# An adaptive-norm feed-forward kernel: the scaling of the down product goes from VectorE to ScalarE and GpSimd

## What is computed

```python
y = conv1d(x, weight, groups=4, padding=4) + cond @ c_weight.T + bias   # 128 x 32 x 512
def qlinear(x, w): return fake_quant(x, axis=-1) @ fake_quant(w, axis=1).T
h = silu(qlinear(y, w_gate)) * qlinear(y, w_up)      # inner width 1376
out = x + qlinear(h, w_down)                         # back to width 512
```

## Time and profile before

| | us |
|---|---|
| median of 3 runs | 334.96 (332.92 to 336.75) |
| the profiled execution, its own time | 334.56 |
| its span, first to last instruction | 332.8 |
| mean granted TensorE clock | 0.981 of full |

### The profile page before, as it was taken

One profiled execution on the slowest core, in us unless ns is written; L12 is line 12 of the kernel. 1 busy time (PEld: TensorE's weight loads), 2 busy tenths in 40 slices (PEclk: granted clock), 3 DMA queues, 4 the chain that ended last, 5 costly groups with the idle time before them and its releaser, 6 DMA issues.

```text
span 332.8 us, 4922 instructions
## 1 busy us (share of the span) xinstructions
PE 298.8 (90%) x1728; PEld 178.5 (54%) x1728; DVE 260.1 (78%) x426; ACT 210.2 (63%) x251; POOL 199.9 (60%) x200
## 2 busy tenths in 40 slices
PE   1989699989639699999999999999999999999934
PEld 1989699986325244444444544444444445444411
DVE  0699998996357678888888888788887888888830
ACT  1057889496975856556766667766577656676530
POOL 1266856793663555776666776657766667756541
PEclk9999799999998999999999999999999999999997
DMA  7899834500000823565445754446654456544482
GB/s 290 325 308 390 306 137 164 220 2 2 0 0 19 196 43 76 136 153 137 110 106 121 141 152 124 108 107 139 152 137 106 108 125 147 147 115 106 111 196 109
DMA packets 59032, 46.36 MB, mean 139 GB/s; under 512 B 47520, under 2 KB 47648, under 8 KB 58112
## 3 DMA queue, kind: packets, MB, share of 16 engines
q1 hardware_dynamic: 58720, 45.43, 48.8%
q10 hardware_dynamic: 288, 0.62, 0.6%
HBM read 26.12 MB, written 8.39 MB: 104 GB/s over the span
## 4 chain that ended last, share of the span: by engine, by line
PE 72%; DVE 14%; ACT 5%; DMA 4%; POOL 1%; issue 1%; SPq 0%; POOLq 0%; ACTq 0%; DVEq 0%
PE bank L765 40%; PE bank L778 21%; PE bank L670 7%; DVE y_part L563 3%; DVE y_mem L554 3%; DMA w_mem<-w_mem 3%; DVE gu_max L531 2%; DMA small_sb<-cond_ctx_bias 2%; ACT y_mem L426 2%; DVE h_max L621 1%; PE bank L726 1%; ACT slab L485 1%; DVE d_max L541 1%; ACT w_mem L494 1%; ACT sg_mem L480 1%
## 5 line engine op out<-in xcount | busy, mean ns | idle before, releaser
L387 POOL TENSOR_TENSOR sg_mem<-sg_mem,gu_scale_row 128x512 f32<-128x512 f32 (+1 forms) x96 | 111.5, 1162 | 88.2 <-ACT sg_mem L480 88.2
L765 PE MATMUL bank<-wgu_t,xq_t 128*128 128x512 bf16 (+1 forms) x768 | 155.8, 359 | 3.8 <-DVE slab L615 3.8
L765 PEld LDWEIGHTS bank<-wgu_t,xq_t 128*128 128x128 bf16 x768 | 75.0, 98 | 82.7 <-DVE slab L615 5.0
L480 ACT ACTIVATE sg_mem<-sg_mem,x_scale 128x512 f32<-128x512 f32 (+1 forms) x96 | 64.3, 672 | 44.9 <-DVE sg_mem L605 44.8
L778 PE MATMUL bank<-wd_t,w_mem 128*128 128x512 bf16 (+1 forms) x352 | 82.8, 385 | 8.7 <-DMA w_mem<-w_mem 8.7
L605 DVE TENSOR_TENSOR sg_mem<-bank,gu_scale_row 128x512 f32<-128x512 f32 (+1 forms) x96 | 60.3, 629 | 31.6 <-PE bank L765 31.6
L615 DVE SCALAR_TENSOR_TENSOR slab<-bank,x_scale,sg_mem 128x512 f32<-128x512 f32 (+1 forms) x96 | 66.5, 692 | 10.0 <-POOL sg_mem L387 9.6
L485 ACT ACTIVATE slab<-slab,h_inv 128x1376 f32<-128x1376 f32 x32 | 46.2, 1443 | 37.2 <-DVE h_inv L521 37.2
L778 PEld LDWEIGHTS bank<-wd_t,w_mem 128*128 128x128 bf16 (+1 forms) x352 | 34.6, 99 | 48.4 <-DMA w_mem<-w_mem 10.0
L670 PE MATMUL bank<-toeplitz,slab 128*128 128x192 f32 (+1 forms) x320 | 54.5, 326 | 0.0
L670 PEld LDWEIGHTS bank<-toeplitz,slab 128*128 128x128 f32 x320 | 51.7, 205 | 0.0
(11 more groups left out here) (44 smaller groups left out, 132.1 us busy)
## 6 DMA issues: line engine op xcount, KB each, us to landing
xo_mem<-x SPq DMA_DIRECT2D x32, 256.0 KB, 3.3
out<-xo_mem SPq DMA_DIRECT2D x32, 256.0 KB, 2.9
w_mem<-w_gate_up SPq DMA_DIRECT2D x10, 512.0 KB, 6.7
slab<-x_blocks SPq DMA_DIRECT2D x4, 1024.0 KB, 8.9
slab<-x_blocks SPq DMA_DIRECT2D x3, 1088.0 KB, 5.9
w_mem<-w_down SPq DMA_DIRECT2D x4, 688.0 KB, 6.4
slab<-x_blocks SPq DMA_DIRECT2D x1, 576.0 KB, 5.1
toeplitz<-taps_wide ACTq DMA_DIRECT2D x1, 512.0 KB, 4.9
```

Of the source, the lines that this page charges most:

```text
L387: pool.tensor_tensor(s, s, gu_scale_row[:, 1, at:at + n], ALU.mult).then_inc(silu_scaled, 1)
L480: act.activation(s, s, ACT.Silu, scale=x_scale[:, i:i + 1]).then_inc(silu_done, 1)
L765: last = pe.matmul(bank[p][:, 0:n], xq_t[:, k, P * i:P * (i + 1)], wgu_t[:, m, k, at:at + n], start=(k == 0), stop=(k == KT - 1))
```

## The change

ACT gets a `scale_down` that reads the down bank and multiplies by the token scale only. It stands between silu(i,0) and silu(i,1) for i from 4 on, and for the last four tiles behind convert_h(31). POOL multiplies `down_out` in place by `wd_scale_row` at the head of `add_residual`, signals a new semaphore `down_rated`, and waits for that semaphore before it adds. DVE's instruction and its waits go.

```diff
             def add_residual(i):
                 t = i % XO_BUFS
+                if i == 0:
+                    pool.wait_ge(xq_copied, len(XQ_USES))
+                pool.wait_ge(down_scaled, i + 1)
+                pool.tensor_tensor(down_out[:, i % 2, :], down_out[:, i % 2, :], wd_scale_row[:, :], ALU.mult)\
+                    .then_inc(down_rated, 1)
                 pool.wait_ge(residual_in[t], 16 * (i // XO_BUFS + 1))
-                pool.wait_ge(down_scaled, i + 1)
+                pool.wait_ge(down_rated, i + 1)
                 pool.tensor_tensor(xo[:, t, :], xo[:, t, :], down_out[:, i % 2, :], ALU.add).then_inc(out_ready, 1)
...
+            def scale_down(i):
+                if i >= 2:
+                    act.wait_ge(out_ready, i - 1)
+                act.wait_ge(h_inv_ready, i + 1)
+                act.wait_ge(down_done, i + 1)
+                act.activation(down_out[:, i % 2, :], down_bank[i % 2][:, :], ACT.Copy, scale=h_scale[:, i:i + 1])\
+                    .then_inc(down_scaled, 1)
+
             for i in range(TILES):
                 silu(i, 0)
+                if i >= LAG + 1:
+                    scale_down(i - LAG - 1)
...
             round_h(TILES - 1)
             convert_h(TILES - 1)
+            for i in range(TILES - LAG - 1, TILES):
+                scale_down(i)
...
-            def scale_down(i):
-                if i >= 2:
-                    dve.wait_ge(out_ready, i - 1)
-                dve.wait_ge(down_done, i + 1)
-                dve.scalar_tensor_tensor(down_out[:, i % 2, :], down_bank[i % 2][:, :], h_scale[:, i:i + 1],
-                                         wd_scale_row[:, :], ALU.mult, ALU.mult).then_inc(down_scaled, 1)
...
-                if i >= LAG + 1:
-                    scale_down(i - LAG - 1)
                 scale_gate(i, 1)
...
             token_scales(TILES - 1)
-            for i in range(TILES - LAG - 1, TILES):
-                scale_down(i)
```

More of the change, by code:

```diff
@@ L170, in adaln_ffn @@
         down_scaled = sem("down_scaled")
+        down_rated = sem("down_rated")
         out_ready = sem("out_ready")
```

## The result

The changed kernel takes 348.67 us (median of 4 runs, 347.85 to 349.59) against 335.35 for the kernel before (4 runs, 332.92 to 336.75): a ratio of 1.041, 95% interval 1.036 to 1.046. It is 13.3 us slower. The forecast was slower by 10.7, 345.7 us, range 341.0 to 350.5. The profiled execution took 347.85 us with a span of 346.1; the span grew by 13.3 as well, so the two traces can be set against each other. In the new file the lines have moved: scale_silu is L388, the multiply L395, the add L399, silu L486, scale_gate L624, multiply_up L634, ScalarE's new copy L508, gate_up L772, down L785.

The account below looks back on a forecast made before the run. PE bounded the kernel before at 7.025 us per tile; a 7.38 us loop through GpSimd would bind after. Span 332.8 + 9.6 (loop) + 1.1 (end) = 343.5, plus 1.76 and 0.4, gives 345.7 us, range 341 to 350.5.

Parts of the forecast that it names:

- PE is the bound before: Middle of the kernel: PE alone sets 7.025 us per tile, so taking 0.74 us per tile off VectorE gains nothing.
- the relief of VectorE keeps GpSimd's part from being worse: VectorE in the loop: its freed time, worth nothing now, would count where VectorE is late through GpSimd's added work.
- ScalarE's copy is hidden: ScalarE between silu(i,0) and silu(i,1): a copy of 0.65 us fits in 0.99 us free, costing 0 in the loop.
- A loop through GpSimd's order: Tile to tile through GpSimd, VectorE and ScalarE, without PE: grows from 6.03 us to over PE's 7.025; chance 0.79.
- Its size, 7.38: Sum of the links from one tile's scale_silu(i,0) to the next's: 0.355 us over PE's tile, 9.6 us in 27 rounds.
- Multiply to add: GpSimd's step from the new multiply to the add, waiting on its own semaphore: 1.35 us, bounds 1.22 and 1.51.
- scale_silu to multiply_up: Link from GpSimd's scale_silu(i,1) to VectorE's multiply_up(i,1), start to start: 1.37 us.
- The end, +1.1: Last four tiles behind convert_h(31): later copies and two GpSimd passes each put the last add 1.1 us later, at most 2.5.
- S'+12.3: Forecast start of down(30), worked out as 12.25 us after the start of GpSimd's first piece of tile 31.
- B: Rival: the tile-to-tile loop stays under PE's 7.025 us, only the end costs, 336.1 us; chance 0.11.
- C: Rival: VectorE is the real bound and its freed 20.7 us count, giving 314 us; chance 0.03.
- D: Rival: every GpSimd wait for itself costs as the kernel's first did, and PE stays slow at the end: 351.4 us; chance 0.07.

Follow-up runs that it names:

- act_copy_only: Changed kernel without GpSimd's multiply by the weight scales, that factor left out of the result; ScalarE's copy stays: 334.72 us, ratio 0.999 to the kernel before.
- dve_scales: Changed kernel with VectorE again scaling the down product out of PSUM instead of ScalarE; GpSimd still multiplies and adds: 347.56 us, ratio 1.037 to the kernel before.
- late_multiply: Changed kernel with GpSimd's multiply and add moved behind scale_silu(i,2), same instructions and engines: 337.54 us, ratio 1.007 to the kernel before.
- gate_first: Changed kernel with scale_gate(i+1,0) ahead of multiply_up(i,1) on VectorE from tile 3 on: 337.41 us, ratio 1.007 to the kernel before.
- rate_256: Changed kernel with GpSimd's multiply over 256 of the 512 columns: 336.25 us, ratio 1.006 to the kernel before.
- rate_384: Changed kernel with GpSimd's multiply over 384 of the 512 columns: 341.65 us, ratio 1.022 to the kernel before.
- spare_pass: Changed kernel with a third, unread 128x512 GpSimd pass ahead of the multiply, residual wait moved before both: 386.46 us, ratio 1.157 to the kernel before.
- late_dve_end: Changed kernel with GpSimd's two passes behind scale_silu(i,2) and the last four tiles scaled on VectorE as before: 334.44 us, ratio 1.001 to the kernel before.
- warm_end: Kernel before, with thirteen unread matmuls on PE between down(30) and down(31): 335.46 us, ratio 1.003 to the kernel before.

## Why the prediction was right, point by point

- *PE is the bound before, and work taken off VectorE is worth nothing.* Right: act_copy_only at 0.999. Its remark that the relief of VectorE keeps GpSimd's part from being worse was not: with VectorE's instruction back (dve_scales) the pace is the same 7.473.
- *ScalarE's copy is hidden.* Right; it took 0.67 us (0.65 was taken), and act_copy_only and dve_scales show from both sides that it has no part in the loss of the loop.
- *A loop through GpSimd's order, longer than PE's tile.* Right in its place and its links: cut on GpSimd (late_multiply) or on VectorE (gate_first), it goes, and it has the threshold at PE's pace (rate_256, rate_384). PE's first stall came in tile 8, as worked out.
- *Its size, 7.38.* This is the term that was too small: 7.473 measured. The prediction had named an added pass of over 1.35 us as a sign that it was wrong, and by that sign its size was. Two links were off. Multiply to add was taken as 1.35, from a pair where GpSimd waits for one semaphore; it was 1.41. Here a second wait, for the residual, stands between the two, and where that wait was moved ahead (spare_pass), 1.36 was measured, the predicted size. As that kernel has a third pass as well, the second wait is the likely cause and not one that was tried alone. And scale_silu to multiply_up was 1.41 and not the 1.37 of the early tile it was read from. 27 rounds cost 12.1 and not 9.6 us; these 2.5 are nearly all of the 2.6 by which the forecast fell short (the end added 0.5, the start took 0.4 off).
- *The end, +1.1, with 2.5 as the bound.* Measured 1.6. Down(30) started where it was forecast (S'+12.3) at half clock, and ended some 0.6 us later than taken, so that GpSimd's third pair came 0.4 late; down(31) had the full clock back, as assumed. The end it is measured against had a slow down(31), which the prediction took from the one trace it had. In late_dve_end's trace, with down(30) slow and down(31) fast, the last add came 19.2 us behind the start of silu(31,0) instead of 21.0, so the cost of the end depends on the execution by about as much as it is worth. late_dve_end, at 1.001, shows that the end was the only cost outside the loop.
- The start, the same code in both, was 0.4 us shorter in this execution.
- *Rivals.* B (the loop stays under PE's tile) is what rate_256 is: 1.006. It was wrong here by 0.45 us per tile. C, VectorE as the bound, falls with act_copy_only. D, a step of 1.51 at every turn, falls with the 1.41 measured.

## What to carry to other kernels

Before work is moved from a busy engine to an idle one, draw the loop that leads from one round to the same place in the next through all engines' fixed orders, and add it up from start to start; an engine at 60% can be the bound if what it does stands between two links of such a loop. Compare this sum with the pace of the bound engine: under it, added work is free, over it each round pays the excess, whatever the busy shares say. If the sum comes out too long, move the added instruction behind the last piece that others wait for, or move the waiting instruction on the other engine behind one that isn't concerned; each brought the loss down from 4.1 to 0.7% here. And look at the end separately, where nothing covers a longer way.

## What was unexpected of the hardware

- What GpSimd pays for waiting on its own semaphore seems to depend on how many waits stand between: the add started 0.08 us after the multiply's end with one wait (spare_pass) and 0.14 with two (changed kernel; 0.15 in rate_384), against a start some 0.03 before the end with none to wait for.
- The granted clock after a pause of PE is not set by the pause alone: behind 2.68 us of idle time, with PE busy at full clock ahead of it, eleven matmuls took 2.55 us at 1.00 in one kernel's trace (before) and 4.22 us at 0.60 in another's (warm_end).
